# Attention kernel: value steps in batches of twenty, transposes grouped 4, 2, 4, PSUM banks split four and three

## The reference

```python
scores = jnp.einsum('ehd,ehd->eh', q[tgt], k[srcidx])
m = jax.ops.segment_max(scores, tgt, num_segments=n)
p = jnp.exp(scores - m[tgt])
s = jax.ops.segment_sum(p, tgt, num_segments=n)
w = p / (s[tgt] + 1e-16)
agg = jax.ops.segment_sum(w[:, :, None] * v[srcidx], tgt, num_segments=n)
```

## Time and profile before

| | us |
|---|---|
| median of 3 runs | 1097.25 |
| lowest and highest run | 1095.75, 1097.47 |
| the profiled execution, its own time | 1096.9 |
| its span in the profile | 1095.1 |
| attention of layer 0, first scores to last value batch | 237.13 to 526.74 |
| attention of layer 1, first scores to last value batch | 688.14 to 977.68 |

### The profile page before, as it was taken

One profiled execution on the slowest core, in us unless ns is written; L12 is line 12 of the kernel. 1 busy time (PEld: TensorE's weight loads), 2 busy tenths in 40 slices (PEclk: granted clock), 3 DMA queues, 4 the chain that ended last, 5 costly groups with the idle time before them and its releaser, 6 DMA issues. The chain is left out here.

```text
span 1095.1 us, 18767 instructions
## 1 busy us (share of the span) xinstructions
PE 1022.3 (93%) x6579; PEld 851.2 (78%) x6579; DVE 763.1 (70%) x2339; ACT 595.4 (54%) x1094; POOL 307.2 (28%) x325
## 2 busy tenths in 40 slices
PE   5899999999999999999899999899999999989853
PEld 3678777887888888887799889788888888869842
DVE  6877557567777777776489710677777777747788
ACT  7634222447666666666334532566666666652366
POOL 2000000014444444443033100344444444422303
PEclk9999999999999999999999999999999999999975
DMA  6232410576412121123103446431211211320403
GB/s 148 63 121 80 130 35 24 134 178 161 104 39 62 39 62 39 39 73 117 59 8 118 97 113 157 109 85 38 62 39 38 62 38 39 114 87 2 94 3 94
DMA packets 50758, 84.98 MB, mean 78 GB/s; under 512 B 15230, under 2 KB 33506, under 8 KB 50412
## 3 DMA queue, kind: packets, MB, share of 16 engines
q1 hardware_dynamic: 50668, 83.82, 30.7%
HBM read 36.50 MB, written 21.61 MB: 53 GB/s over the span
## 5 line engine op out<-in xcount | busy, mean ns | idle before, releaser
L1299 POOL TENSOR_SCALAR probs<-probs,mass_inv 125x1250 f32<-125x1250 f32 x160 | 210.7, 1317 | 344.0 <-DVE mass_inv L1426 344.0
L1417 DVE CUSTOM_DVE_ANT_0 probs<-banks,scores_bias 125x416 f32<-125x416 f32 (+1 forms) x480 | 267.4, 583 | 46.1 <-PE banks L1319 41.8
L1319 PE MATMUL banks<-k_stack,q_stack 128*125 128x416 f32 (+1 forms) x960 | 294.6, 392 | 2.4 <-DVEq L1404 2.4
L1333 PE MATMUL banks<-ident,probs 125*125 125x125 f32 x1600 | 258.6, 276 | 8.1 <-DVE probs_t L1408 5.9
L1333 PEld LDWEIGHTS banks<-ident,probs 125*125 125x125 f32 x1600 | 240.5, 187 | 32.0 <-issue 22.3
L1387 ACT ACTIVATE probs<-probs,neg_peak 125x1250 f32<-125x1250 f32 x160 | 213.4, 1334 | 54.7 <-DVE neg_peak L1440 54.7
L1374 ACT ACTIVATE probs_t<-banks 125x500 f32<-125x500 f32 x320 | 152.3, 477 | 108.0 <-PE banks L1333 108.0
L1348 PE MATMUL banks<-probs_t,v_pair 125*64 125x250 f32 x1600 | 186.2, 379 | 0.9 <-ACT probs_t L1374 0.9
L1319 PEld LDWEIGHTS banks<-k_stack,q_stack 128*125 128x125 f32 x960 | 143.8, 188 | 30.7 <-issue 16.6
L1348 PEld LDWEIGHTS banks<-probs_t,v_pair 125*64 125x64 f32 x1600 | 107.4, 136 | 54.4 <-ACT probs_t L1374 1.3
L1408 DVE COPY probs_t<-banks 125x500 f32<-125x500 f32 x160 | 108.2, 676 | 54.5 <-PE banks L1333 54.5
(11 more groups left out here) (257 smaller groups left out, 1407.9 us busy)
## 6 DMA issues: line engine op xcount, KB each, us to landing
q_stack<-q_split SPq DMA_DIRECT2D x160, 125.0 KB, 2.3
scores_bias<-edge_bias SPq DMA_DIRECT2D x8, 1171.9 KB
edge_bias<-bias_row SPq DMA_DIRECT2D x10, 585.9 KB
k_stack<-k_lo SPq DMA_DIRECT2D x16, 312.5 KB, 4.4
resid<-residual SPq DMA_DIRECT2D x2, 2500.0 KB, 9.9
values<-v_stage SPq DMA_DIRECT2D x2, 1680.0 KB
residual<-t SPq DMA_DIRECT2D x4, 625.0 KB, 3.0
xs<-in_x SPq DMA_DIRECT2D x5, 480.0 KB
```

The source lines that it names most:

```text
L1299: nc.gpsimd.tensor_scalar(probs[:, u % 4, :], probs[:, u % 4, :], mass_inv[:, u % 4:u % 4 + 1], 1.0, ALU.mult, ALU.mult).then_inc(att["pro ...
L1319: mm = nc.tensor.matmul(pb[0:NT, t % 5, 0:sn], q_stack[:, n % 2, half, part, tile * NT:(tile + 1) * NT], k_stack[:, head * N + s0:head * N ...
L1333: mm = nc.tensor.transpose(pb[0:NT, 5 + t % 2, j * NT:(j + 1) * NT], probs[:, u % 4, (j0 + j) * NT:(j0 + j + 1) * NT], ident[0:NT, 0:NT])
L1417: nc.vector.tensor_tensor_reduce(out=probs[:, slot % 4, s0:s0 + sn], in0=pb[0:NT, t % 5, 0:sn], in1=scores_bias[:, (n % GROUPS) * GROUP + ...
```

## The change

The three groups of transposes of a unit hold 4, 2 and 4 tiles in place of 4, 4 and 2, so VectorE copies two tiles and ScalarE twice four. The score chunks rotate through four banks (0 to 3), the transposes through three (4 to 6), one for each group of a unit; a group now waits for the copy of the same group one unit before. All twenty value steps of a pass stand in one batch, at slot 7 behind the start of the pass. `out_of` comes one slot after it, and the list has two slots fewer. The numbers of `s_free` that SyncE waits for fall by one with the bank.

```diff
--- before.py
+++ after.py
@@ -432,9 +432,9 @@
 
         PASSES = PAIRS * GROUPS
         UNITS = 4 * PASSES
-        PARTS = ((0, 4), (4, 4), (8, 2))
+        PARTS = ((0, 4), (4, 2), (6, 4))
         T_LAG, PV_LAG = 3, 7
-        PV_BATCHES = {0: range(0, TILES), 2: range(TILES, 2 * TILES)}
+        PV_BATCHES = {0: range(0, 2 * TILES)}
         SLOTS = 4 * (PASSES - 1) + PV_LAG + max(PV_BATCHES) + 1
         part_engine = (0, 1, 0)
 
@@ -455,7 +455,7 @@
                 if part_engine[i] == e and (j0, jn) in parts:
                     n, half, tile = unit(u)
                     copy(3 * u + i, probs_t[:, n % 2, half, j0:j0 + jn, tile * NT:(tile + 1) * NT],
-                         pb[0:NT, 5 + (3 * u + i) % 2, 0:jn * NT].rearrange("p (j n) -> p j n", j=jn))
+                         pb[0:NT, 4 + i, 0:jn * NT].rearrange("p (j n) -> p j n", j=jn))
 
         def split(pool, n):
 
@@ -471,7 +471,7 @@
 
             sp.wait_ge(att["q_split"], n + 1)
             if n >= 2:
-                sp.wait_ge(att["s_free"], 5 + 12 * (n - 1))
+                sp.wait_ge(att["s_free"], 4 + 12 * (n - 1))
             for half in range(2):
                 own = slice(half * DH, half * DH + DH)
                 for to in (slice(0, DH), slice(DH, 2 * DH)):
@@ -1286,7 +1286,7 @@
                             values(c + 1)
 
                     sp.dma_start(resid[:, :, :], res_d).then_inc(oph["res"], 16)
-                    sp.wait_ge(att["s_free"], 5 + 3 * UNITS)
+                    sp.wait_ge(att["s_free"], 4 + 3 * UNITS)
                     sp.dma_start(wo_nat[:, :, :], weight(gnn["Wo"], DC)[:, ds(layer * DC, DC), :]).then_inc(oph["wo"], 16)
                     sp.dma_start(w1_nat[:, :, :], weight(gnn["W1"], FC)[:, ds(layer * FC, FC), :]).then_inc(oph["w1"], 16)
                     sp.dma_start(w2_nat[:, :, :], weight(gnn["W2"], DC)[:, ds(layer * DC, DC), :]).then_inc(oph["w2"], 16)
@@ -1316,7 +1316,7 @@
                         (s0, sn), t = CHUNKS[i], 3 * slot + i
                         pe.wait_ge(att["s_free"], t + 1)
                         for part in range(2):
-                            mm = nc.tensor.matmul(pb[0:NT, t % 5, 0:sn],
+                            mm = nc.tensor.matmul(pb[0:NT, t % 4, 0:sn],
                                                   q_stack[:, n % 2, half, part, tile * NT:(tile + 1) * NT],
                                                   k_stack[:, head * N + s0:head * N + s0 + sn], start=part == 0, stop=part == 1)
                         mm.then_inc(att["s_ready"], 1)
@@ -1326,11 +1326,11 @@
                         if i == 0:
                             pe.wait_ge(att["probs"], u + 1)
                         (j0, jn), t = PARTS[i], 3 * u + i
-                        if t >= 2:
-                            e = part_engine[(t - 2) % 3]
-                            pe.wait_ge(att[f"t_free{e}"], freed(e, t - 1))
+                        if t >= 3:
+                            e = part_engine[i]
+                            pe.wait_ge(att[f"t_free{e}"], freed(e, t - 2))
                         for j in range(jn):
-                            mm = nc.tensor.transpose(pb[0:NT, 5 + t % 2, j * NT:(j + 1) * NT],
+                            mm = nc.tensor.transpose(pb[0:NT, 4 + t % 3, j * NT:(j + 1) * NT],
                                                      probs[:, u % 4, (j0 + j) * NT:(j0 + j + 1) * NT], ident[0:NT, 0:NT])
                         mm.then_inc(att["t_ready"], 1)
 
@@ -1401,7 +1401,7 @@
 
                 @block.vector
                 def _(dve):
-                    dve.sem_inc(att["s_free"], 5)
+                    dve.sem_inc(att["s_free"], 4)
 
                     def copy(t, to, of):
                         dve.wait_ge(att["t_ready"], t + 1)
@@ -1415,7 +1415,7 @@
                         (s0, sn), t = CHUNKS[i], 3 * slot + i
                         dve.wait_ge(att["s_ready"], t + 1)
                         nc.vector.tensor_tensor_reduce(
-                            out=probs[:, slot % 4, s0:s0 + sn], in0=pb[0:NT, t % 5, 0:sn],
+                            out=probs[:, slot % 4, s0:s0 + sn], in0=pb[0:NT, t % 4, 0:sn],
                             in1=scores_bias[:, (n % GROUPS) * GROUP + tile, s0:s0 + sn], scale=1.0, scalar=-3e38,
                             op0=ALU.add, op1=ALU.max, accum_out=peak[:, slot % 4, i:i + 1]).then_inc(att["s_free"], 1)
 
@@ -1436,7 +1436,7 @@
                         if slot < UNITS:
                             scored(slot, 1)
                             scored(slot, 2)
-                            dve.wait_ge(att["s_free"], 5 + 3 * slot + 3)
+                            dve.wait_ge(att["s_free"], 4 + 3 * slot + 3)
                             nc.vector.tensor_reduce(neg_peak[:, slot % 4:slot % 4 + 1], peak[:, slot % 4, :], AX.X, ALU.max,
                                                     negate=True).then_inc(att["neg_peak"], 1)
```

## The result

The changed kernel takes 1149.39 us in the median of four runs (1145.07 to 1150.97), the kernel before 1097.11 in the same comparison: a ratio of 1.0471, interval 1.0446 to 1.0497. It is slower by 52.3 us; 1150 was forecast. The profiled execution is the quickest of the four, 1145.07 us with a span of 1143.3, so what its trace shows accounts for 48 of the 52 us.

The account below looks back on a forecast made before the run. TensorE, 93% busy, bounds the kernel; under it lies a hidden 3.05 us round per slot that rules after the change. 36 x 1.44 = 51.8, plus 2 x 0.8, make 53.4; 1096.9 + 53.4 = 1150.3 us, range 1142 to 1161.

Parts of the forecast that it names:

- The round of 3.05 us: Exponential, mass, chunk 1, maximum, next exponential: no slot can be shorter than 3.05 us, though TensorE could take 2.23.
- The exponential held behind the batch: ScalarE issues the first transposes' copy before the exponential, so after a value batch the exponential starts only at 1.60 us.
- The wait for the bank behind chunk 1: With four banks, a slot's last score pair waits for the previous slot's chunk 1; TensorE restarts 0.12 us after release.
- The way from the last wait to the batch's end: From the last score pair's start, 10.12 us, through transposes and batch entry, to the value batch's end at 15.50 us.
- 1.44 us per pass: A pass takes 15.50 us against 14.06; times 36 passes in two layers, 51.8 us.
- TensorE's own work: Per pass 4 x 2.23 + 0.19 + 4.38 = 13.49 us, 0.57 less than today.
- Start and end of a layer: An estimated 0.2 us more before the first batch and 0.6 more in the tail, 0.8 per layer.
- The bounds: 1143 to 1160 us, from uncertainties in the score pair's restart, the read terms and the tail; forecast within them 86%.
- the clock's fall: Rival: TensorE's standstills lower its clock, a pass's 13.49 us become 20.2, kernel time 1320 us; chance 2%.
- the unchanged bound: Rival: TensorE stays the bound, no bank wait is met, each pass takes 13.49 us, kernel time 1076 us; chance 4%.
- the release one chunk earlier: Rival: scores are let go one chunk earlier than counted, 0.64 us more per pass, kernel time 1120 us; chance 5%.
- the cancelling of cover and cost: Rival: the 0.20 us wait and one batch entry are traded for one bank wait, within 0.2% of 1097; chance 1%.

Follow-up runs that it names:

- four banks alone: The kernel before with four score banks in place of five, nothing else: 1095.80 us, ratio 0.9991.
- two tens: The changed kernel with its values in two batches of ten as before, new groups and banks kept: 1111.00 us, ratio 1.0117.
- the kernel in which neither the round nor the order on ScalarE holds anything: Changed kernel with inversion last, groups 2, 4, 4, VectorE copying the first, ScalarE the others after its exponential: 1067.06 us, ratio 0.9725.

## Why the prediction was right

The forecast was 1150.3 us from the profiled execution of before, 1149.39 was measured. By its steps:

- **The round of 3.05 us.** Right to the hundredth: 401.42, 404.47, 407.52, 410.57. That it rules the three slots without value work is shown by the inversion moved to the end (1149 to 1081 us) and back (1067 to 1103).
- **The exponential held behind the batch.** Right: it starts 1.60 us after the batch's end (415.28 to 416.88). Freed in two steps it gave 47 us, with the groups changed too, and then 12 us by itself.
- **The wait for the bank behind chunk 1.** It stands where it was forecast, but the restart was put 0.06 us too high. I had let the next load start 0.12 us after a release, as after VectorE's copy. Measured: the chunk of 406.20, its read from 406.69 to 406.77, the load at 406.83. That is 0.06 us (the two timelines of the changed kernel above). My three starts at 4.02, 7.07 and 10.12 us behind the batch's end came at 3.96, 7.01 and 10.06 (403.78, 406.83, 409.88 less 399.82). It also explains the two misses of 5 us, four banks alone and two tens.
- **The way from the last wait to the batch's end.** 10.12 to 15.50 forecast, 5.38 us; 409.88 to 415.28 measured, 5.40.
- **1.44 us per pass.** Measured 15.46 less 14.06, 1.40, in the passes shown. In the mean of the 18 passes of layer 1 it is 15.44 (732.45 to 1010.45) less 14.07 (709.23 to 962.53), 1.37; 36 times, 49.4 for 51.8.
- **TensorE's own work.** The 0.57 us by which it was said to fall are two things: by the prediction's terms two batches of ten make 4 x 2.23 + 2 x (0.19 + 2.26) = 13.82 us, so 0.33 us are the entry and exit of a batch, and 0.24 us the two waits for VectorE's copy.
- **Start and end of a layer.** Forecast 0.8 us per layer more. Start: 21.11 us from the first scores to the first batch before (237.13 to 258.24), 21.27 now (235.16 to 256.43), 0.16. End: from the batch at 962.53 to the last one are 10.70 us before, from 1010.45 to the last one 10.89 now, where 11.3 was forecast: my chain by POOL came to 0.4 too much. The rows:

```profile
1010.45 4.45 PE L1348 MATMUL banks<-probs_t,v_pair 125*64 125x250 f32 x40
...
1019.31 1.35 PE L1333 MATMUL banks<-ident,probs 125*125 125x125 f32 x10 [0.61 <-POOL probs L1299]
1021.34 4.45 PE L1348 MATMUL banks<-probs_t,v_pair 125*64 125x250 f32 x40 [0.68 <-ACT probs_t L1374]
```

- **The sum.** 49.4 us for the passes, 0.3 for the two starts and 0.4 for the two ends make 50.1. The attention of layer 1 takes 314.59 us (711.20 to 1025.79) for 289.54, 25.05 more, and so 50.1 for two layers as well. The runs differ by 52.3 us in the median; the profiled execution by 48.2, as its stage before the attention was 2.0 us shorter. The 2.2 us between 50.1 and 52.3 are within the spread of the four runs (5.9 us) and aren't located. The forecast was 53.4, in steps that were each a little too high, 3.3 us together. That the median lies within a microsecond of 1150 is in part luck: the 2.2 us that aren't located make up for most of this.
- **The bounds.** The lower one adds up all the uncertainties (4, 2 and 1.5 us, to 1143); the upper one has only the 9 us of the restart (1160). With the others added it would be 1163. The measured time lies inside either.
- **VectorE's shorter copy gains nothing, ScalarE's longer ones cost nothing.** The first is borne out: VectorE waits 0.66 us for the exponential before the mass row of 405.93, where it waited 0.43. The second holds in its time (0.67 us of idle before each exponential that is not behind a batch), but the groups weren't neutral: the four transposes in front of the batch cost some 8 us against two (of the 9.5 by which that run was faster), which the prediction had in its chain (0.51 us) without saying that it was a cost of the change.
- **What the profile after was to show.** Waits of 0.4, 0.8 and 0.8 us at the scores: 0.23, 0.74 and 0.74. TensorE busy 87% of a pass: wrong, its matmul rows cover 14.32 of 15.46 us, 93%. The rows leave 1.14 us idle in a pass in which the loads wait 1.71 us and stand still for 0.38 more behind the batch, so the waits are to be read from the loads. ScalarE's wait for a value batch is 2.93 us, where over 3 was forecast. Clock 1.00: so it was.

Of the rivals, the clock's fall and the unchanged bound are refuted by the window above. So is the release one chunk earlier, which would have made a pass 14.70 us, and the cancelling of cover and cost, which needed two of the three waits to be absent. The Trainium skill (Perfetto Trace Analysis, Identifying the Most-Contended Engine) has one optimise the engine with the highest occupancy, and judges TensorE by its weight loads. By either measure this is TensorE here (93% and 78%, VectorE 70%). This case's answer is that behind it stood a round between VectorE and ScalarE that was only 0.5 us per slot short of ruling (3.05 of 3.52 us): the longer batch alone cost 43 us, and the 0.57 us a pass that was reckoned came only in the kernel in which neither the round nor the order on ScalarE holds anything (13.49 us). How much of that is the longer batch's isn't shown: no run has that kernel with two batches of ten, and with the inversion last alone the batch's length made no difference (1080.80 and 1080.64). The advice of the Trainium skill (Perfetto Trace Analysis, Matmul Optimizations), to use all eight banks, isn't borne out here by itself: with seven in use the kernel before took the same time (0.9991).

## What to carry to other kernels

In a loop in which several engines work through lists of their own, look for the closed round (here maximum, exponential, mass, next chunks) and time it where nothing covers it, as in the first slots; lumping the work of the engine that seems full takes away the cover of the slots that lose theirs. Then look at which instruction each member of the round stands behind: one move of two VectorE instructions of under 0.2 us each was worth 68 us in the changed kernel, and 5 in the kernel before. Judge a regrouping by what stands behind the last instruction that waits, not by the busy time that it moves between engines.

## What the runs showed of the hardware

Entering and leaving the value matmuls has a price that no wait in the trace explains. There are 0.19 us more in front of a batch than in front of a score pair, and 0.38 us without weight loads behind it, with batches of 20 rows and of 40. Not all of the 0.38 us is lost: two batches of 20 take 2 x 2.26 us, one of 40 takes 4.38, so an exit costs 0.14 us and a batch less saves 0.33.

TensorE's granted clock stayed at 1.00 in the passes of the changed kernel, though the loads waited 1.7 us of each 15.5. In all fourteen traces it was 0.99 to 1.00 from 240 to 510 us and from 705 to 940.

A wait of TensorE for a VectorE chunk was over 0.06 us after the read of its accumulator ended, half of what one for a VectorE copy took (0.12).

The stage before the attention, which no edit touches, differed by up to 3.8 us between the fourteen profiled executions (first scores between 235.1 and 238.9 us). That limits what a single profile can say of small gains.
